# Attention outputs kept feature by query, two heads to a strip, denominators by a second pass with ones

## The reference, cut to what matters

```python
q = heads(layernorm(x) @ Wq.T + bq); k = heads(ctx @ Wk.T + bk); v = heads(ctx @ Wv.T + bv)
# layer 0 applies a rotary embedding to q and k; layer 1 adds a mask row
attn = softmax(einsum('bhsd,bhtd->bhst', q, k) / 4, axis=-1)
out = einsum('bhst,bhtd->bhsd', attn, v).transpose(0, 2, 1, 3).reshape(B, S, E)
x = x + out @ Wo.T + bo
x = x + experts(layernorm(x))       # untouched by the change
```

## Time and profile before

| | |
|---|---|
| three runs, device us | 983.6, 984.75, 990.06; median 984.75 |
| profiled execution | 988.88 us, its span 987.1 us |
| PE, DVE, ACT, POOL busy | 878.9 (89%), 656.6 (67%), 483.6 (49%), 379.9 (38%) us |
| mean granted TensorE clock | 0.958 of full speed |
| layer 0 attention loop | about 46 to 168 us of the span |
| layer 1 attention loop | about 551 to 661 us of the span |
| experts of the two layers | the stretches behind each |

### The profile page before, as it was taken

One profiled execution on the slowest core, in us unless ns is written; L12 is line 12 of the kernel. 1 busy time (PEld: TensorE's weight loads), 2 busy tenths in 40 slices (PEclk: granted clock), 3 DMA queues, 4 the chain that ended last, 5 costly groups with the idle time before them and its releaser, 6 DMA issues.

```text
span 987.1 us, 21017 instructions
## 1 busy us (share of the span) xinstructions
PE 878.9 (89%) x7941; PEld 768.0 (78%) x7941; DVE 656.6 (67%) x1367; ACT 483.6 (49%) x809; POOL 379.9 (38%) x390
## 2 busy tenths in 40 slices
PE   5688888974899999999956899989899999999997
PEld 4577776752789999999944788867788888888886
DVE  6876776540457777777758556766966666666666
ACT  3666568510336677676634665685222222222221
POOL 4353344067106888888750322220212212121210
PEclk9799999985899999999988999999999999999999
DMA  7029020024236888888661000110010100010002
GB/s 207 23 67 284 29 71 2 1 86 151 90 124 167 235 226 231 237 230 222 173 154 44 24 2 2 35 34 1 17 33 16 32 16 32 16 32 16 16 1 86
DMA packets 46112, 85.43 MB, mean 87 GB/s; under 512 B 6240, under 2 KB 33120, under 8 KB 45920
## 3 DMA queue, kind: packets, MB, share of 16 engines
q0 software_dynamic: 14784, 46.44, 17.4%
q1 hardware_dynamic: 31264, 38.09, 12.8%
HBM read 63.73 MB, written 20.79 MB: 86 GB/s over the span
## 4 chain that ended last, share of the span: by engine, by line
PE 71%; DVE 10%; ACT 8%; issue 6%; POOL 3%; DMA 2%; DVEq 0%; SPq 0%; ACTq 0%; POOLq 0%
PE bank L1398 38%; PE bank L1434 12%; PE bank L1493 5%; PE bank L1607 3%; PE bank L1654 2%; PE bank L1583 2%; ACT prob L730 2%; PE bank L1688 2%; PE bank L1664 1%; DVE low_f L1220 1%; DMA ctx_raw<-in_ctxT 1%; DVE xres L1091 1%; DVE xT_lo L907 1%; PE bank L1387 1%; PE bank L1459 1%
## 5 line engine op out<-in xcount | busy, mean ns | idle before, releaser
L1101 DVE TENSOR_TENSOR hid<-bank,act_sb 128x512 f32<-128x512 f32 x88 | 60.8, 691 | 147.0 <-ACT act_sb L661 127.0
L661 ACT ACTIVATE act_sb<-bank 128x512 f32<-128x512 f32 x88 | 52.5, 597 | 204.8 <-PE bank L1398 164.2
L1398 PE MATMUL bank<-xT_hi,w_hi 128*128 128x512 f32 x352 | 141.3, 402 | 7.9 <-issue 4.8
L1398 PE MATMUL bank<-xT_hi,w_lo 128*128 128x512 f32 x352 | 141.4, 402 | 6.8 <-issue 6.6
L1398 PE MATMUL bank<-xT_lo,w_hi 128*128 128x512 f32 x352 | 141.5, 402 | 5.7 <-issue 5.7
L1091 DVE SCALAR_TENSOR_TENSOR xres<-bank,gate,xres 128x256 f32<-128x256 f32 x320 | 132.7, 475 | 1.4 <-PE bank L1434 1.4
L404 POOL TENSOR_TENSOR w_hi<-w_raw,zero_col 128x768 fp32r<-128x768 f32 (+1 forms) x20 | 31.9, 1595 | 243.7 <-PE bank L1434 239.0
L1398 PE MATMUL bank<-xsT_hi,w_hi 128*128 128x256 f32 x368 | 105.7, 287 | 2.2 <-DVE xsT_lo L1058 1.5
L1434 PE MATMUL bank<-w_hi,hid_hi 128*128 128x256 f32 x352 | 102.1, 290 | 5.8 <-DVE hid_lo L1106 5.8
L472 POOL DMA_INDIRECT summed<-y_sb,tile_to x46 | 94.9, 2064 | 27.1 <-issue 12.7
L1434 PE MATMUL bank<-w_lo,hid_hi 128*128 128x256 f32 x352 | 101.1, 287 | 3.0 <-issue 3.0
(11 more groups left out here) (207 smaller groups left out, 2196.9 us busy)
## 6 DMA issues: line engine op xcount, KB each, us to landing
w_raw<-in_fw SPq DMA_DIRECT2D x18, 384.0 KB, 3.0
sorted_x<-empty_row SPq DMA_DIRECT2D x2, 2967.0 KB, 19.8
xs<-sorted_x SPq DMA_DIRECT2D x23, 258.0 KB
ctx_raw<-in_ctxT SPq DMA_DIRECT2D x8, 512.0 KB, 4.7
summed<-empty_row SPq DMA_DIRECT2D x1, 2304.0 KB, 26.7
xres<-in_x SPq DMA_DIRECT2D x4, 512.0 KB, 6.9
xn_all<-summed SPq DMA_DIRECT2D x4, 512.0 KB, 5.8
out_x<-xres SPq DMA_DIRECT2D x4, 512.0 KB, 3.0
```

Source lines behind the costliest of these rows:

```text
L661: nc.scalar.activation(act_sb[:, r, :], bank[2 * r + 1][:], ACT.Silu).then_inc(f["act"], 1)
L1101: nc.vector.tensor_tensor(hid[:, r, :], bank[2 * r][:], act_sb[:, r, :], ALU.mult).then_inc(f["hid"], 1)
L1398: last = nc.tensor.matmul(dst, lh, rh, start=(i == 0), stop=(i == len(pairs) - 1))
```

## The change

A bank of outputs stays feature by query. A strip of 32 partitions now holds the 16 value features of two heads: `v_full` is laid out so that reading 32 columns at one offset gives values and then zeros, and at another zeros and then values, and the two heads' products add up in one strip. A second pass over the same exponentials with ones in place of values (`sum_cols`) gives each feature row its denominator, in the bank's other half. VectorE takes the reciprocal of that half, 128x256, and multiplies into `oT` directly. The two copies of ScalarE and the six transposes are gone. The output weights are loaded in eight pieces of 16 rows, in the order of the strips. Projection and residual come one batch earlier, the residual behind the output in VectorE's order; `scores(b)` waits for the residual of b - 4; the first `low` after the loop moves behind the last residual.

```diff
-        v_full = sb(at, "v_full", [P, 2, BLK, HEADS, VW], F32)
+        v_full = sb(at, "v_full", [P, 2, BLK, GRP, VG], F32)          # VG = GRP * VW + HD = 144
-        rden = sb(at, "rden", [P, 2, HEADS], F32)
+        sum_cols = sb(at, "sum_cols", [P, 2, VW], F32)
+        rden = sb(at, "rden", [P, 2, D], F32)
...
         def wo_bank(b):
-            return 3 if b == B - 2 else 2
+            return 2 if b == B - 1 else 1
...
-                sp.dma_start(aw_out[:].rearrange("p k d -> p (k d)"), aw[l][:, OUT_FROM[l], :]).then_inc(a["aw_in2"], 16)
+                for q in range(GRP):
+                    for h in range(2):
+                        at_row, from_row = VW * q + HD * h, HD * (GRP * h + q)
+                        sp.dma_start(aw_out[at_row:at_row + HD].rearrange("p k d -> p (k d)"),
+                                     aw[l][from_row:from_row + HD, OUT_FROM[l], :]).then_inc(a["aw_in2"], 16)
...
-                pool.wait_ge(a["vset"], 1)
-                nc.gpsimd.memset(v_full[:, :, :, :, HD], 1.0).then_inc(a["vset"], 1)
+                nc.gpsimd.memset(sum_cols[:], 0.0).then_inc(a["vset"], 1)
                 pool.wait_ge(a["vset"], 2)
+                for h in range(2):
+                    nc.gpsimd.memset(sum_cols[:, h, HD * h:HD * (h + 1)], 1.0).then_inc(a["sums"], 1)
...
-                        if b >= 1:
-                            output_copy(b - 1)
-                        if b >= 2:
-                            output_turned_copy(b - 2)
...
                 def output(b):
-                    dve.wait_ge(a["oback"], b + 1)
-                    back = bank[0][:].rearrange("p (h w) -> p h w", w=VW)
-                    nc.vector.reciprocal(rden[:, b % 2, :], back[:, :, HD]).then_inc(a["rden"], 1)
+                    dve.wait_ge(a["pv"], b + 1)
+                    nc.vector.reciprocal(rden[:, b % 2, :], bank[0][:, D:2 * D]).then_inc(a["rden"], 1)
                     dve.wait_ge(a["rden"], b + 1)
-                    nc.vector.tensor_tensor(o_sb[:, b % 2], back[:, :, 0:HD],
-                                            rden[:, b % 2].unsqueeze(2).to_broadcast([P, HEADS, HD]),
+                    nc.vector.tensor_tensor(oT[:, b % 2].rearrange("p k t -> p (k t)"), bank[0][:, 0:D], rden[:, b % 2, :],
                                             ALU.mult).then_inc(a["o"], 1)
...
-                        if b >= 3:
-                            residual(b - 3)
                         if b >= 1:
                             output(b - 1)
+                        if b >= 2:
+                            residual(b - 2)
...
-                    residual(B - 3)
                     output(B - 1)
-                    low(2 * l + 1, 0)
                     residual(B - 2)
                     residual(B - 1)
+                    low(2 * l + 1, 0)
...
                     if b >= 3:
                         pe.wait_ge(a["o"], b - 2)
                     if b >= 4:
-                        pe.wait_ge(a["ocopied"], b - 3)
-                    if b >= 5:
-                        pe.wait_ge(a["xadd"], b - 4)
+                        pe.wait_ge(a["xadd"], b - 3)
...
-                    for pair in range(2):
+                    strips = v_full[:, n % 2, c].rearrange("p g w -> p (g w)")
+                    for sums in range(2):
                         for u in range(KT):
-                            for q in range(4):
-                                r, j = 2 * pair + q // 2, q % 2
-                                last = nc.tensor.matmul(bank[0][32 * q:32 * q + VW, S * (2 * u + pair):S * (2 * u + pair + 1)],
-                                                        v_full[:, n % 2, c, 8 * u + 2 * r + j, :],
-                                                        prob[:, b % 2, r, S * (2 * u + j):S * (2 * u + j + 1)],
-                                                        start=True, stop=True)
+                            for h in range(2):
+                                for q in range(GRP):
+                                    r, j = 2 * h + q // 2, q % 2
+                                    at_strip = 2 * VG * u + GRP * VW * h + VW * q
+                                    left = sum_cols[:, h, :] if sums else strips[:, at_strip:at_strip + VW]
+                                    at_col = D * sums + S * u
+                                    last = nc.tensor.matmul(bank[0][VW * q:VW * (q + 1), at_col:at_col + S], left,
+                                                            prob[:, b % 2, r, S * (2 * u + j):S * (2 * u + j + 1)],
+                                                            start=(sums == 0 and u == 0 and h == 0),
+                                                            stop=(sums == 1 and u == KT - 1 and h == 1))
...
-                def turned_back(b):
-                def output_turned(b):
                 def projected(b):
-                    pe.wait_ge(a["ocopied"], b + 1)
-                    pe.wait_ge(a["max"], NG * (b + 4) + 3 if b + 4 < B else NG * B)
+                    pe.wait_ge(a["o"], b + 1)
+                    pe.wait_ge(a["max"], NG * (b + 3) + 2 if b + 3 < B else NG * B)
...
-                            output_turned(b - 2)
-                        if b >= 3:
-                            projected(b - 3)
-                        if b >= 1:
-                            turned_back(b - 1)
+                            projected(b - 2)
```

More of the change, by code:

```diff
@@ L19 @@
 VW = 32
+VG = GRP * VW + HD
 E0, E1 = 8, 16
@@ L115, in program @@
         ident_bf = sb(at, "ident_bf", [P, P], BF16)
[L116 removed]
+        at_pad = sb(at, "at_pad", [P, 128], F32)
         unit_raw = sb(at, "unit_raw", [P, 2, N], F32)
         at_gap = sb(at, "at_gap", [P, 3112], F32)
[L119 to L121 removed]
+        pick = sb(at, "pick", [P, GRP, P], BF16)
+        sum_cols = sb(at, "sum_cols", [P, 2, VW], F32)
+        rden = sb(at, "rden", [P, 2, D], F32)
+        o_pad = sb(at, "o_pad", [P, 736], F32)
         oT = sb(at, "oT", [P, 2, KT, P], F32)
@@ L189, in program @@
                           "proj", "raw", "rope", "rot", "q0set", "q1set", "kk", "vps", "vset", "v",
-                          "score", "max", "low3", "lowT", "lowset", "lowcopy", "turn", "exp", "pv", "ocopy", "oback", "rden", "o",
-                          "oT", "ocopied", "wo", "xadd", "xbo"], l)
+                          "score", "max", "low3", "lowT", "lowset", "lowcopy", "turn", "exp", "pv", "rden", "o", "sums", "wo", "xadd", "xbo"], l)
               for l in range(2)]
@@ L1643, in weighed @@
                     pe.wait_ge(a["exp"], NG * (b + 1))
+                    if b == 0:
+                        pe.wait_ge(a["sums"], 2)
                     if c == 0:
@@ L1658, in weighed @@
-                    last.then_inc(a["pv"], 1)
-                def turned_back(b):
-                    pe.wait_ge(a["ocopy"], b + 1)
-                    for g in range(NG):
-                        last = nc.tensor.transpose(bank[0][:, S * g:S * (g + 1)], o_turned[:, b % 2, S * g:S * (g + 1)],
-                                                   ident[:])
-                    last.then_inc(a["oback"], 1)
-                def output_turned(b):
+                            for h in range(2):
[8 more added lines that the diff above has]
+                                                            stop=(sums == 1 and u == KT - 1 and h == 1))
@@ L1670, in output_turned, with projected @@
+                    last.then_inc(a["pv"], 1)
+                def projected(b):
                     pe.wait_ge(a["o"], b + 1)
                     pe.wait_ge(a["max"], NG * (b + 3) + 2 if b + 3 < B else NG * B)
-                    if b >= 1:
-                        pe.wait_ge(a["ocopied"], b)
-                    for k in range(KT):
-                        src = o_sb[:, b % 2, 8 * k:8 * (k + 1), :].rearrange("p h d -> p (h d)")
-                        last = nc.tensor.transpose(bank[1][:, P * k:P * (k + 1)], src, ident[:])
@@ L1677, in output_turned @@
-                    last.then_inc(a["oT"], 1)
-                def projected(b):
-                    pe.wait_ge(a["ocopied"], b + 1)
-                    pe.wait_ge(a["max"], NG * (b + 4) + 3 if b + 4 < B else NG * B)
-                    if b >= 1 and b != B - 2:
+                    if 1 <= b < B - 1:
                         pe.wait_ge(a["xadd"], b)
                     if b == 0:
-                        pe.wait_ge(a["aw_in2"], 16)
+                        pe.wait_ge(a["aw_in2"], 16 * 2 * GRP)
```

25 lines of the change are left out of this document (5 added, 20 removed).

## The result

The changed kernel took 1000.33 us (median), the kernel before beside it on the same chip 984.84: a ratio of 1.0135, 95% interval [1.0101, 1.0169], or 13.3 us slower (one disturbed run is in the median and not in the ratio; without it the median is 998.53). A second comparison on another chip gave 1005.07 against 989.13, ratio 1.0167 [1.0135, 1.0199]. The forecast was 1008 and a difference of 22.8 us. The sign, the operation that decides and the place where most of the cost falls were right. The size was 6 to 10 us too large, by the one comparison or the other.

What follows compares the result with a forecast made beforehand. Output latency over three engines was taken to bound twelve blocks, not TensorE's work. 13.6 + 2.8 + 3.4 + 1 + 2 = 22.8 us slower, on the median 984.75, gave 1008; range 996 to 1018, 1021 with a falling clock.

Steps and rivals of the forecast that it cites:

- the rival "cheap": Attention loops: a wide reciprocal streams like a product, 0.42 us, so only +4 us, 989 us in all; chance 0.10.
- The twelve blocks: Batches 10 to 13 of layer 0, 1 to 4 and 10 to 13 of layer 1: 13.6 us slower together.
- the ring: Loop through weighing, reciprocal, product and residual to the next scores, whose latency bounds twelve batches: +1.5 us each.
- the gaps: In twelve batches, time between the product's end and the scores waiting for it: 4.4 us together, subtracted from the cost.
- The fourteen others: Remaining batches 1 to 13, with key, query and value units between: 0.2 us each on the mean, 2.8 us.
- TensorE's sum is 0.04: nothing: TensorE per batch: 1.10 us more weighing, less 0.62 and 0.44 of removed transposes, leaves 0.04 us.
- all 3.4 us count: Layer 1's opening: seven more weight-load issues send the context load out 3.4 us later, and all of it costs time.
- the queue is otherwise quiet: Layer 0's opening: SyncE's queue has little else, so the later context load was taken to cost 1 us.
- The ends: After each loop: last output's chain about 0, subtractions moved behind the last residual 1 us a layer, 2 us together.
- this rival: Eight late batches of both layers: TensorE's idle stretches drop its clock to 1.2 GHz, adding 13 us, 1020; chance 0.15.
- the proportional rival: Attention loops: the reciprocal grows with its columns to 4.1 us, VectorE bounds all 26 batches, +60 us, 1070; chance 0.04.
- Freeing ScalarE: Attention loops: 1 us less on ScalarE and no turning back pull the loop forward by over 10 us; chance 0.03.

Runs made afterwards that it cites:

- e1: The changed kernel with the 128x256 reciprocal replaced by a plain multiplication of the same shape: 959.6 us against 956.72, ratio 1.0027.
- e2: The kernel before with a second, 256-column reciprocal added, its result written over at once: 982.81 us against 956.72, ratio 1.0279.
- e8: The changed kernel with a plain multiplication for the reciprocal and the second pass (ones) left out: 975.35 us against 989.13, ratio 0.9882.
- e10: The kernel before with its output weights loaded in eight pieces of 16 rows instead of one: 958.63 us against 958.14, ratio 1.0016.
- e4: The changed kernel with VectorE's residual put back ahead of the output: 997.5 us against 956.72, ratio 1.043.
- e6: The changed kernel with one weight load, the ones pass first and in bank 1, projection in bank 2: 1007.23 us against 989.13, ratio 1.0194.

## Why the prediction was right in kind and too large

**The reciprocal.** Forecast 1.88 us from two rows with 4 and 16 columns; measured 1.75. A column cost (1752 - 256) / 240 = 6.2 ns, not 6.75. The two other prices, 0.42 and 4.1, were far off, so the row nearest in kind was the right guide, and the rival "cheap" fell with it. That this operation is what makes the change slower is shown by e1 from one side (1.0027 without it) and by e2 from the other.

**The twelve blocks** grew by 3.7 us (layer 0, blocks 10 to 13), 1.4 (layer 1, 1 to 4) and 4.5 (10 to 13): 9.7 us against 13.6. The step that failed is the price of the ring, "+1.5 us a block", not the count or the gaps (by the trace these add up to 4.3). From the start of the weighing to the scores the prediction had 5.1 us; it was 4.71 (640.36 to 645.07), so a block pays 1.15. Of the 0.4 us, 0.26 lie in the weighing (2.02 us until the reciprocal starts, where 2.28 was forecast: the second pass begins 0.89 us behind the first, not 1.10), 0.12 in the reciprocal, and the rest behind it. With 1.15 in the same sum, 12 x 1.15 - 4.4 = 9.4, and 9.7 was measured.

**The fourteen others** grew by 3.0 us, with 2.8 forecast: the number was right by luck, the reason was wrong. The prediction had VectorE arrive late at the items' operations because of the reciprocal. But with the cheap operation of e1 these blocks are as long as after, and without the pass (e8) the ones of layer 0 below are 0.7 to 0.9 us shorter. It is TensorE's own work that bounds them, and "TensorE's sum is 0.04: nothing" was the mistaken step. In blocks 7 to 9 of layer 0 the turning back, with its copies, was worth 0.5 to 0.6 us (8.3 to 7.8, 8.2 to 7.6, 7.8 to 7.2, before against e8) and not the 1.06 of its records, and the pass costs 0.7 to 0.9 and not 1.10.

**The openings.** The step "all 3.4 us count" was too large: 2.0 us by the means with one load and with eight. The load did go out 3.25 us later (3.73 against 0.48), but was read 1.2 us sooner after its issue (1.4 in e10). Layer 0 was given 1 us and shows nothing of it. Its context load was issued at 20.28 instead of 19.39, 0.9 us later and not 3.4. The seven issues fell into a stall of the queue: the constants' issue at L302 held it 5.84 us before and 3.39 after, so the prediction's "the queue is otherwise quiet" was wrong there.

**The ends.** Up to the last residual they changed by -0.8 and 0.0: the wide costs and the removed copies and turns cancelled, as the prediction said. The little gain in layer 0 has no experiment that says its cause. The one us a layer for the late `low` was right, but lies behind the last residual, outside the table. Layer 1, before and after:

```profile
660.85 0.42 DVE L1236 TENSOR_TENSOR xres<-bank,xres 128x256 f32<-128x256 f32 x1 [1.36 <-PE bank L1688]
...
666.38 0.50 PE L1398 MATMUL bank<-xT_hi,w_hi 128*128 128x512 f32 x1
```

```profile
670.12 0.42 DVE L1224 TENSOR_TENSOR xres<-bank,xres 128x256 f32<-128x256 f32 x1 [0.96 <-PE bank L1661]
...
671.89 0.39 PE L1705 MATMUL bank<-xT_hi,route_wr 128*32 128x512 f32 x1 [1.00 <-DVE xT_lo L896]
...
676.70 0.50 PE L1385 MATMUL bank<-xT_hi,w_hi 128*128 128x512 f32 x1
```

The router's first product waits 1.00 us for that subtraction, and the experts' first product starts 6.6 us behind the last residual instead of 5.5. Layer 0 shows the same, and so do all kernels here with either order. With it the ends cost 1.3 us, where 2 were forecast.

**The sum:** 9.7 + 3.0 + 2.0 + 0 + 1.3 = 16.0 us, and 13.3 and 16.5 were measured (each ratio times the kernel before beside it). Of the 6.8 us too many in the forecast, 3.9 lay in the ring, 2.4 in the openings and 0.7 in the ends, less 0.2 in the fourteen blocks. The sum can't be held to a microsecond: between the two layers' attention, where the change adds only the late `low`, the profiled after was 2.4 us shorter than before and the one of the second comparison 2.8 longer.

**The other rivals.** The clock did not fall as this rival had it, in all eight late blocks for 13 us. The profiled windows have 0.98 and 1.00, though TensorE sat idle 1.64 us at a stretch, and the scores behind that wait took 1.20 us, against 1.17 before. It fell in one late block of the second comparison, at 0.9 us, and often in e4. The column that cost 6.2 ns sets the proportional rival aside. Freeing ScalarE did not pull the loop forward: of the 26 blocks only one is over 0.1 us shorter after (block 1 of layer 1, 6.70 against 7.02).

## What to carry to other kernels

Before a small operation is made wide to spare a layout change, its cost per column has to be taken from rows of that very operation; a reciprocal is not a copy, and here sixteen times the columns cost seven times the time. Where a loop alternates between blocks bound by one engine's work and blocks bound by a ring over several, each edit has to be priced twice: the reciprocal cost time only in the ring and the ends, the pass with ones in both kinds of block. A bank that is freed earlier for one user makes another wait: e6 won 10 us of VectorE's waiting and lost it to one reduction more ahead of TensorE.

## What the runs showed of the hardware that was not expected

- The reciprocal took 145 to 256 ns for 4 to 16 columns and 1752 ns for 256. The Trainium skill (VectorE: DVE Perf Modes, "Walkthrough: the 8-slice pipeline in each mode") has it as an iterative divide with a repeat count of eight; the estimate from it, 2.1 us, was 0.35 above the measured time.
- TensorE's matmuls become shorter at a time that differs between executions of nearly the same program. In the opening of layer 0 the same matmuls go from 0.63 us each to 0.39 at about 17.2 us before and by 14.6 after. The granted clock reads 1.00 on both sides, so only the durations show this:

```profile
15.57 0.63 PE L1398 MATMUL bank<-ctx_hi,aw_lo 128*128 128x512 f32 x1
...
17.23 0.39 PE L1398 MATMUL bank<-ctx_lo,aw_hi 128*128 128x512 f32 x1
```

```profile
14.59 0.39 PE L1385 MATMUL bank<-ctx_hi,aw_lo 128*128 128x512 f32 x1
```

  Up to 13.4 us the engine had done the same work at the same times, within 0.05 us. The opening was 1.7 us shorter, and 38.9 again in the comparison on another chip; so one opening of one profile says nothing about an edit of that size.
- How long TensorE sat idle does not settle whether its clock is lower behind it. The scores of the earlier trace rows took 2.09 us behind a wait of 2.44 us. In e10, whose loops are the same program, they took 1.17 behind 2.43, and the granted clock fell only behind them, at about 132.6 us. The changed kernel kept its clock behind 1.64 us and lost it behind 1.47.

```profile
131.18 1.17 PE L1585 MATMUL bank<-k_full,q_half 32*128 32x128 f32 x32 [2.43 <-ACT q_half L703]
```

- In the opening of layer 1 the load of 512 KB behind eight small ones landed sooner after its own issue (5.1 to 5.5 us in six profiles) than behind one load of the same bytes (5.7 to 6.9 in six). So a later issue is not a landing later by as much.
